# The down side's high product in one matmul per rank with its regrouping by copies between partitions, and the residual bias of the first units at other times

## The reference

```
x = x + layernorm(x) * scan(ctx*ctx)          # r = 0.9 r + kv over the tokens
h = layernorm(x) @ W_exp + b_exp              # 512 -> 2048
h = butterfly(h, up_weights)                  # 11 stages, stage s pairs i with i xor 2^s
h = gelu(h + up_bias)
h = butterfly(h, down_weights)                # 11 stages
x = x + h @ W_con + b_con + down_bias         # 2048 -> 512
```

## Time and profile before

| | us |
|---|---|
| median of 3 runs | 2752.51 (2751.94 to 2758.26) |
| the profiled execution | 2752.11, its span 2750.4 |
| PE busy in the span | 2728.7 |
| first product starts | about 114 |
| second pair starts | 139.6 |

### The profile page before, as it was taken

The page is one execution under the profiler, slowest core; times in us unless marked ns, Lnnn a source line. Parts: engine busy times, 40 slices in busy tenths (PEclk is TensorE's granted clock), DMA queues, the critical chain, the costliest instruction groups (busy, mean ns, idle before and its releaser), DMA issues.

```text
span 2750.4 us, 35138 instructions
## 1 busy us (share of the span) xinstructions
PE 2728.7 (99%) x12168; PEld 2251.9 (82%) x12168; DVE 2119.6 (77%) x3544; ACT 1132.2 (41%) x1731; POOL 427.1 (16%) x608
## 2 busy tenths in 40 slices
PE   8999999999999999999999999999999999999998
PEld 6788888888888888888888888888888888888887
DVE  8888887877878777787877788787787877778533
ACT  5754434344343433434343343434334343343432
POOL 5356010110101011020111101011010101102000
PEclk8999999999999999999999999999999999999999
DMA  9675956657585675857657585675758567585543
GB/s 274 244 235 171 281 165 198 200 170 224 155 231 177 181 220 161 241 153 216 194 168 222 152 249 165 194 202 171 223 156 235 172 189 213 161 242 153 187 146 100
DMA packets 288373, 535.76 MB, mean 195 GB/s; under 512 B 36854, under 2 KB 98454, under 8 KB 271046
## 3 DMA queue, kind: packets, MB, share of 16 engines
q1 hardware_dynamic: 281808, 531.05, 64.1%
q10 hardware_dynamic: 5414, 1.25, 0.3%
q0 software_dynamic: 976, 1.22, 0.2%
HBM read 437.96 MB, written 63.96 MB: 182 GB/s over the span
## 4 chain that ended last, share of the span: by engine, by line
PE 98%; DVE 1%; ACT 0%; issue 0%; DMA 0%; POOL 0%; DVEq 0%
PE ps L1916 44%; PE ps L1937 25%; PE ps L1950 25%; PE ps L1814 1%; PE ps L1710 1%; PE ps L1782 0%; PE ps L1818 0%; PE ps L1812 0%; PE ps L1824 0%; DMA wexp<-in_L_ffn_W_exp_dram 0%; PE ps L2022 0%; PE ps L1803 0%; DVE raw L1462 0%; DVE xop L1445 0%; PE ps L1729 0%
## 5 line engine op out<-in xcount | busy, mean ns | idle before, releaser
L1916 PE MATMUL ps<-xop,w1r 128*128 128x512 f32 x5376 | 1366.1, 389 | 2.4 <-DVE xop L1445 2.4
L1916 PEld LDWEIGHTS ps<-xop,w1r 128*128 128x128 f32 x5376 | 1009.0, 188 | 215.2 <-DVE xop L1445 3.4
L1937 PE MATMUL ps<-w2r,ghi 128*128 128x512 f32 x2048 | 630.5, 389 | 0.0
L1950 PE MATMUL ps<-w2r,ghi 128*128 128x512 f32 x2032 | 625.7, 389 | 1.1 <-DVE x L1544 1.1
L1127 ACT ACTIVATE st<-ps 128x512 f32<-128x512 f32 x384 | 229.6, 598 | 820.0 <-PE ps L1916 819.9
L1544 DVE TENSOR_TENSOR x<-ps,x 128x512 f32<-128x512 f32 x508 | 348.4, 686 | 275.1 <-PE ps L1950 272.7
L1937 PEld LDWEIGHTS ps<-w2r,ghi 128*128 128x128 f32 x2048 | 384.4, 188 | 79.9 <-DVE w2x L1341 0.2
L1950 PEld LDWEIGHTS ps<-w2r,ghi 128*128 128x128 f32 x2032 | 381.3, 188 | 81.0 <-DVE x L1544 2.0
L1562 DVE TENSOR_TENSOR g<-ps,st 128x512 f32<-128x512 f32 x384 | 262.5, 684 | 211.7 <-PE ps L1916 211.7
L1131 ACT ACTIVATE g<-g,gelu_bias 128x512 f32<-128x512 f32 x384 | 275.5, 717 | 353.0 <-DVE g L1562 352.9
L1567 DVE TENSOR_TENSOR glo<-g,ghi 128x512 fp32r<-128x512 f32 x510 | 350.9, 708 | 72.8 <-ACT ghi L1145 72.8
(11 more groups left out here) (182 smaller groups left out, 1700.0 us busy)
## 6 DMA issues: line engine op xcount, KB each, us to landing
w1r<-w_products SPq DMA_DIRECT2D x847, 256.0 KB, 3.3
w2r<-w_split SPq DMA_DIRECT2D x126, 1024.0 KB, 5.0
x<-in_x_dram SPq DMA_DIRECT2D x128, 256.0 KB, 7.0
raw<-kv SPq DMA_DIRECT2D x480, 64.0 KB, 2.1
out_dram<-x SPq DMA_DIRECT2D x120, 256.0 KB, 4.1
kv<-in_ctx_dram SPq DMA_DIRECT2D x64, 256.0 KB, 7.4
raw<-in_ctx_dram SPq DMA_DIRECT2D x64, 256.0 KB, 5.0
w_products<-w1r SPq DMA_DIRECT2D x43, 256.0 KB, 6.9
```

The lines of the kernel that those rows point to most:

```text
L1916: last = nc.tensor.matmul(bank[:, :], w1r[:, slot, w, c * P:(c + 1) * P], xop[:, XPOS[m], v, c, :], start=(opens and i == 0), stop=(i == l ...
L1937: last = nc.tensor.matmul(ps_ya[j][:, :], g[:, p % 2, q, j * P:(j + 1) * P], w2r[:, p % 2, kk, w, :], start=(p == 0 and kk == 0 and i == 0 ...
L1950: last = nc.tensor.matmul(ps_yb[:, :], g[:, p % 2, q, j * P:(j + 1) * P], w2r[:, p % 2, kk, w, :], start=(kk == 0 and i == 0), stop=(kk == ...
```

## The change

- `high_dn` r becomes one 128x512 matmul with HX[:, 1, r] stationary; its rows come out as (half, e, k), and ACT keeps it as Z[:, r, :]. `turn_high` and `top_products` change their layouts to fit.
- The 64 `back` transposes and their 16 copies out of PSUM go. In their place SP issues 32 DMAs from Z to wcon (`move_dn`): for each r one with blocks 0 to 7, from 64 partitions, and one with blocks 8 to 15. Each carries 128 KB in rows of 2 KB, and lands in eight partitions, r, r+16, ..., r+112.
- On SP the first 16 stand behind group 0 of `store_w1(0)` and a wait for `high_dn` 7; group 1 goes in the middle of them; group 2, the load and `store_w1(1)` stand behind all 32.
- `low_dn` 0 waits for all first-half moves, `low_dn` 6 for all others. `tokens_hi` with xop slot s below 4 waits for the moves out of Z's rows 4s to 4s+3.
- Fold order on PE: 16 `high_dn`, `tokens` 0 to 3, `bias_low`, `turn_low`, `bias_turn`, `low_dn` 0 and 1, `tokens` 4 to 7, `low_dn` 2 and 3, products 0 and 1, `low_dn` 4 to 7, product 2.
- POOL: the adds in the middle of unit 0 are two for unit 0's first rows; the other two stand at the end of unit 0; then POOL waits for the first product of unit 1, and adds unit 1's second rows and first rows.

```diff
+            def move_dn(blocks, r, moved):
+                wait_kept(sp, "high_dn", r)
+                sp.dma_start(wcon[r:P:R, blocks, :], Z[blocks.start * E:blocks.stop * E, r, :]).then_inc(moved, NX)
...
-            store_w1(0)
+            store_w1(0, range(1))
+            sp.wait_ge(fold_made, fold_at("high_dn", R // 2 - 1) + 1)
+            for r in range(R):
+                move_dn(slice(0, KH // 2), r, dn_low_moved)
+                if r == R // 2:
+                    store_w1(0, range(1, 2))
+            sp.wait_ge(fold_made, fold_at("high_dn", R - 1) + 1)
+            for r in range(R):
+                move_dn(slice(KH // 2, KH), r, dn_top_moved[r // 4])
+            store_w1(0, range(2, NG))
...
-                add_bias(2, 0, x, (0, 1))
+                add_bias(0, 0, xs[0], (0, 1))
                 late_lo(4, (4, 5, 6))
-                add_bias(2, 0, x, (2, 3))
...
+                add_bias(0, 0, xs[0], (2, 3))
+                pool.wait_ge(m_done, PER + 1)
                 add_bias(3, 1, x)
-                add_bias(0, 0, xs[0])
+                add_bias(2, 0, x)
...
+                if first and XSLOT[m] < R // 4:
+                    act.wait_ge(dn_low_moved, R * NX)
+                    act.wait_ge(dn_top_moved[XSLOT[m]], 4 * NX)
+                if first and m == 6:
+                    act.wait_ge(w1_stored[0][2], NX)
...
                 if kind == "low_dn":
                     k = W2_ORDER[i]
-                    wait_kept(pe, "back", k)
+                    if i == 0:
+                        pe.wait_ge(dn_low_moved, R * NX)
+                    if i == LOW_BLOCKS_FIRST:
+                        for moved in dn_top_moved:
+                            pe.wait_ge(moved, 4 * NX)
...
+                if kind == "high_dn":
+                    nc.tensor.matmul(bank[:, :], HX[:, 1, i, :], wcon[:, i, :], start=True, stop=True).then_inc(fold_made, 1)
+                    return
...
-                        last = nc.tensor.transpose(o, Zd[:, c, i * P:(i + 1) * P], ident[:, :])
```

More of the change, by code:

```diff
@@ L205, in xattn_ffn_program @@
         ps_f = ps[5:8]
+        dn_low_moved = sem("dn_low_moved")
+        dn_top_moved = [sem(f"dn_top_moved{q}") for q in range(R // 4)]
         low_loaded = [sem("low_up_loaded"), sem("low_dn_loaded")]
@@ L325, in xattn_ffn_program @@
         FOLD += [("turn_high", q, "act") for q in range(R // 4)]
-        FOLD += [("high_dn", r, "act") for r in range(4)]
+        FOLD += [("high_dn", r, "act") for r in range(R)]
+        FOLD += [("tokens", i, "act") for i in range(J)]
         FOLD += [("bias_low", 0, "act")]
-        FOLD += [("high_dn", r, "act") for r in range(4, 8)]
+        FOLD += [("turn_low", q, "act") for q in range(KH // 4)]
         FOLD += [("bias_turn", 0, "act")]
[L330 to L341, removed]
+        FOLD += [("low_dn", k, "dve") for k in range(2)]
+        FOLD += [("tokens", i, "act") for i in range(J, 2 * J)]
+        FOLD += [("low_dn", k, "dve") for k in range(2, KH)]
         kept_count, kept_so_far = [], {"act": 0, "dve": 0}
@@ L443, in kept @@
                     whole.rearrange("p (a e r) -> p a r e", a=4, e=E)
[L444 to L448, removed]
+            assert kind == "tokens"
+            return raw[:, i // J, :, :].rearrange("p c (g j i) -> p c g j i", g=G, j=J)[:, :, :, i % J, :],\
+                whole.rearrange("p (c g i) -> p c g i", c=KD, g=G)
         def w2_slot(i):
@@ L1088, in _ @@
             weights_hi(1)
-            fold_step("high_dn", 3)
-            fold_step("bias_low", 0)
-            for r in range(4, 8):
+            for r in range(3, R):
                 fold_step("high_dn", r)
[L1093 to L1096, removed]
             for group in range(2):
                 act.wait_ge(w1_stored[0][group], NX)
-            for i in range(2):
+            for i in range(J):
                 fold_step("tokens", i)
[L1101 to L1104, removed]
+            tokens_hi(0, 0, True)
+            fold_step("bias_low", 0)
+            tokens_hi(0, 1, True)
             for q in range(KH // 4):
                 fold_step("turn_low", q)
[L1107 to L1111, removed]
-                fold_step("tokens", i)
[L1113 to L1117, removed]
+            fold_step("bias_turn", 0)
+            for k in range(2):
+                fold_step("low_dn", k)
+            for i in range(J, 2 * J):
+                fold_step("tokens", i)
+            for k in range(2, 4):
                 fold_step("low_dn", k)
@@ L1320, in top_products @@
                     coef = spread_view(ps[bank][:, :], 0, LOW - 1, KH // 4)
[L1321 to L1328, removed]
+                    last = path_stage(nc.vector, flat(whole), paths, coef, LOW - 1)
                 last.then_inc(low_matrix_ready, 1)
@@ L1507, in _ @@
                 normalise(0, 1, xs[0], j)
-            for k in (11, 13):
-                fold_step("back", k)
-            for i in range(J + 2, 2 * J):
-                fold_step("tokens", i)
             tokens_lo(0, 0)
             tokens_lo(0, 1)
-            token_sum(0, 0, first=True)
             for k in range(2):
                 fold_step("low_dn", k)
+            token_sum(0, 0, first=True)
             token_sum(0, 1)
@@ L1816, in fold_step @@
                         last = nc.tensor.transpose(o, HX[:, 1, 4 * i + c, :], ident[:, :])
-                    elif kind == "high_dn":
-                        last = nc.tensor.matmul(o, wcon[:, i, block_c], HX[:, 1, i, :], start=True, stop=True)
                     elif kind == "turn_low":
@@ L1877, in _ @@
                 fold_step("turn_low", q)
-            wait_kept(pe, "high_dn", R - 2)
-            wait_kept(pe, "high_dn", R - 1)
-            for k in range(KH):
-                if k == 10:
-                    for i in range(J, J + 2):
-                        fold_step("tokens", i)
-                fold_step("back", k)
-            for i in range(J + 2, 2 * J):
+            fold_step("bias_turn", 0)
+            wait_kept(pe, "turn_low", KH // 4 - 1)
+            for k in range(2):
+                fold_step("low_dn", k)
+            for i in range(J, 2 * J):
                 fold_step("tokens", i)
-            wait_kept(pe, "turn_low", KH // 4 - 1)
             def product(u, p, m, first):
```

46 lines of the change are left out of this document (19 added, 27 removed).

## The result

| | before | after |
|---|---|---|
| median of the runs | 2752.2 us (4 runs, 2751.4 to 2758.3) | 2766.7 us (4 runs, 2764.3 to 2768.8) |
| ratio | | 1.0049, 95% interval 1.0033 to 1.0065 |
| profiled execution | 2752.1 us, span 2750.4 | span 2765.1 |
| PE busy | 2728.7 us | 2727.4 us |
| mean granted clock | 0.996 | 0.993 |

The changed kernel is 14.4 us slower; 2762 was forecast. PE's busy time is what it was: fewer matmuls, some of them at the lower clock. The time went into waits.

A forecast was written before the change was run, and what follows sets the result against it. PE's own work was taken as the bound, so the price is almost wholly the second pair's shift from 139.6 us. 2752.1 + 7.8 (late product 2) + 2.5 (clock) - 0.5 (bias) = 2761.9, so 2762 us; range 2756 to 2770.

The forecast's parts named there:

- both ranges: Of the kernel's time: the forecast's own range, 2756 to 2770 us, and the wider one, 2745 to 2770 us.
- The step by which T was found: Time per 128 KB copy into eight partitions: the middle in ratio between bounds of 0.57 and 2.3 us.
- The back transposes gone: Fold on PE: the 64 transposes took 7.8 us by summed row, some 7.4 by pitch, with nothing hiding them.
- T = 1.15: Copies from Z to wcon: 1.15 us for each 128 KB copy, at 115 GB/s.
- the 91 us of the formula: Copies' landing times: the n-th copy lands at about 91 + nT, all by 127.8 us.
- The first wait: At low_dn 0, ready at 104.4: it waits 5 us for the first half of the copies, landing at 109.4.
- The second wait: At low_dn 6: it waits 8.6 us for all copies to land, at 127.8.
- The clock, 2.5 us: Behind the 8.6 us pause of PE: lower clock (1.2 GHz) for the first microseconds, bounds nothing to 3.5 us, 2.5 taken.
- Product 2: Start of the second pair: 131.5 us instead of 123.72, 7.8 us late, before the clock term.
- The stores behind the copies cost nothing: Stores queued behind the copies (2.8 MB): needed only by second-pair loads 20 us later, so costed at nothing.
- The bias, -0.5: POOL's adds around unit 1's first products: bounds -1.1 and +1.9 us, -0.5 taken.
- The rival of the fast copies: Copies at the x loads' pace (T = 0.57 or 0.64), no wait at low_dn 6: 2746 us; chance 0.28.

The follow-up runs named there:

- run 3: The whole change, but each copy lands in eight partitions four apart instead of sixteen apart: 2755.4 us (1.0012 to the kernel before).
- run 5: The whole change, but each copy lands in eight neighbouring partitions, only the time being read: 2776.7 us (one run).
- run 7: The whole change, with store group 1 issued ahead of the first copy instead of behind the ninth: 2768.0 us (1.0059 to the kernel before).
- run 12: The whole change, with four of the next unit's eight x loads issued one pair later: 2765.1 us (1.0045 to the kernel before).
- runs 4 and 6: 4: the change, but regrouping by way of DRAM, 2751.9 us (0.9999); 6: the change, each copy moving only half the columns, 2753.7 us.

## Why the prediction was right, and where it was off

- *Verdict and mechanism.* Slower was the likelier side (0.52), and the cause is the one given: copies into eight partitions sixteen apart are slow, and the seventh `low_dn` waits for them. The 2766.7 measured lies in both ranges, 4.7 us above the forecast. The step by which T was found was lucky all the same: it is the middle between a pace that eight partitions have as well as 32 and one that goes with their number, and run 3 shows that the number sets nothing here (eight partitions four apart, 178 GB/s).
- *The back transposes gone.* L1824 isn't there; PE is busy 1.3 us less in all; of the other 6.5 us, 4.3 went into matmuls at half pace (see *The clock*) and 1.1 into the first 80 us, ahead of the change; for the last 1.1 us no row was found.
- *The pace, T = 1.15.* 118 GB/s in a window of copies alone is 1.11 us, and 111 over the longer one is 1.18; from the 91 us of the formula to 131.2 it is 1.26 each. The last copies landed 3.4 us after the predicted 127.8. The first was issued at 90.5 and not 88.5, which is 2.0 of it. The rest isn't the copies' own pace: by 116 us 114 GB/s since 90 us had moved some 20.6 of them (an estimate, the store taken off), and the other 11.4 took 15.1 us, 1.3 each, beside the stores issued behind them. The sum had those stores wait their turn; no run held them back, so that they slowed the copies is likely and not shown. By the Trainium skill (SBUF — State Buffer, "Door 1: The DMA port swizzle") four ports give 109 GB/s; the trace has 111 to 118. Its eight ports for four apart (218 GB/s) are not contradicted by run 3 (178, with an issue that allows 175); two of its ports for eight neighbours (54 GB/s) are: run 5 has 71 to 107. The order of the three is as the rule says, and that it is places, not number, that counts is what run 3 showed.
- *The first wait.* Predicted at `low_dn` 0 (5 us). It came earlier on PE, before `bias_low`, as 6.2 us. The step that failed is "ACT waits for the store in the midst of the copies ...; that lands near 102": it landed at 104.6, 8.1 us after issue, where the same store without a copy ahead of it took 4.6 (run 7). I had seen the wait and its place, and not that the bank which ACT frees there is needed by `bias_low`. Run 7 shows that it made no difference to the end: with the store ahead the wait is where I had it, and the time is no better.
- *The second wait.* Predicted 8.6 us, released by a DMA at `low_dn` 6; 6.2 us measured, with PE's arrival 5.8 us late (125.0 against 119.2, from the first wait and its clock) and the copies 3.4 us late.
- *The clock, 2.5 us.* The lower level (1.2 GHz) came behind both waits, where I had granted it to the second alone: `bias_low` took 2.6 us longer and two `low_dn` steps 1.7 us longer, 4.3 in all. But the 2.6 us only made PE later for copies that it waited 6.2 us for anyway, and product 2 stands behind the first of the two steps, `low_dn` 6, which took 2.06 us against some 0.9. So the term is worth 1.2 us in the sum, and 2.5 was too much. Product 2 itself ran at full pace (1.66 us).
- *Product 2.* 131.5 and then 2.5 for the clock make 134.0; measured 136.1: the copies 3.4 us later than predicted, the clock 1.3 less. Two errors that partly cancel.
- *The stores behind the copies cost nothing.* This is the term that was wrong: the waits are 2.9 us, of which run 12 gave back 1.7 in its span. The cover that I counted to 20 us (loads of the second pair) holds; but these stores push later ones, the x loads and then the late weights, and at 190.9 a load issued 13.1 us before is what PE waits for. The engines are full from 130 to 190 us in the changed kernel (shares 0.98 to 1.08), in the kernel before only to 170 (1.04 from 160, then 0.37). I looked at the first user of the delayed stores, and not at the end of the queue that they delay.
- *The bias, -0.5.* PE's waits there fell from 1.1 us to 0.5. Right in the profile, below what the runs can show.
- *The sum.* 9.8 predicted, 14.7 measured in spans: 12.4 at product 2 instead of 10.3, and 2.9 instead of 0 at 194 us, less 0.6.
- *The rival of the fast copies.* Its condition (no wait for copies) was made true by runs 4 and 6, and its gain did not come: 2751.9 and 2753.7 where it said 2746. Product 2 was early as worked out (118.3) or nearly (120.5), and what lies behind it, waits for the late weights and matmuls at the lower clock, took that back. That rival should have carried a later time, near 2752. With it fails what the prediction starts from, that behind product 2 everything goes at PE's and DVE's own pace, so that the price is by how much the second pair starts earlier or later: for a later start it held but for 2.3 us, for an earlier one it did not hold.

## What to carry to other kernels

Before a shuffle between partitions is given to the DMA engines, ask which partitions it lands in, not only how many bytes it has: copies of the same size took 1.1 us, at most 0.75, or some 1.5 by their target partitions alone. A stretch in which the transfers are idle is also a stretch that lets later backlog shrink; whoever delays what stood in it should look for the price at the last load of the backlog, here 60 us on. Price a stall of PE with what may come behind it: a spell at the lower clock cost some 2 us in five of these executions, and nothing where PE had to wait again anyway. And an early start gained on PE is worth only as much as the next wait behind it allows: follow the moved point to the end of the crowded stretch before it is entered as a gain.

## What was not expected of the hardware

- The DMA engines' busy share doesn't tell whether they are fast: from 106 to 114 us shares of 0.51, 0.53 and 0.54 went with 178, 118 and 97 GB/s, in run 3, the change and run 5.
- In a queue with narrow copies ahead, a store of 256 KB took 8.1 us to land against 3.8 with faster copies (run 3), and 1 MB took 18.4 against 6.6.
- The way by DRAM and back, 8 MB in 32 transfers from or to 128 partitions, was quicker than 4 MB in 32 copies within SBUF into partitions sixteen apart: with it no `low_dn` waited for a transfer.
